# First stage: the transposes of the probabilities ahead of the projection of the values

## What is computed

```python
h = _layernorm(x) * (1 + ca) + sa          # per batch element
# attention: 16 heads of 64, window of 32 keys back
xn = rms_norm(h); q, k, v = split(xn @ w_qkv.T)
q, k = apply_rope(q), apply_rope(k)
attn = softmax(where(0 <= q_pos - k_pos <= 32, q.k / 8, NEG))
x = x + ga * ((attn @ v) @ w_out.T)
```

## Time and profile before

| | |
|---|---|
| median of 3 runs | 1226.2 us (1223.17 to 1226.77) |
| profiled execution, span | 1223.0 us (no other time is given for it) |
| TensorE busy | 1102.8 us, 90% |
| VectorE busy | 971.2 us, 79% |
| ScalarE busy | 921.4 us, 75% |
| GpSimd busy | 854.5 us, 70% |
| mean granted TensorE clock | 0.942 |

### The profile page before, as it was taken

How to read it: one execution, slowest core, us unless ns; L and a number is a source line. 1 busy time by engine, 2 the same in 40 slices (tenths; PEclk the granted TensorE clock), 3 DMA queues, 4 the chain that set the end, 5 groups by cost and what they waited for, 6 DMA issues and landing times. The chain is left out here.

```text
span 1223.0 us, 49591 instructions
## 1 busy us (share of the span) xinstructions
PE 1102.8 (90%) x17489; PEld 902.1 (74%) x17489; DVE 971.2 (79%) x4190; ACT 921.4 (75%) x3404; POOL 854.5 (70%) x685
## 2 busy tenths in 40 slices
PE   4899999999999999999999999947999984599992
PEld 2688888888888888888888887725787773488882
DVE  6898998898898898988989987546788764188884
ACT  2689989989889899899899898836776752366661
POOL 2777877877877878777878776554576677067775
PEclk9899999999999999999999999969988885699996
DMA  6766666766666666667667667352243123676110
GB/s 197 208 166 167 177 169 164 182 166 168 175 167 170 177 167 170 176 156 183 166 170 175 163 156 188 96 184 80 62 137 103 55 81 135 172 196 178 58 37 22
DMA packets 111026, 180.88 MB, mean 148 GB/s; under 512 B 19726, under 2 KB 64177, under 8 KB 110656
## 3 DMA queue, kind: packets, MB, share of 16 engines
q1 hardware_dynamic: 102944, 158.53, 50.3%
q0 software_dynamic: 6400, 16.82, 3.8%
q10 hardware_dynamic: 1440, 2.36, 0.8%
HBM read 35.20 MB, written 24.73 MB: 49 GB/s over the span
## 5 line engine op out<-in xcount | busy, mean ns | idle before, releaser
L612 POOL TENSOR_TENSOR qk<-mm,sw 128x1024 f32<-128x1024 f32 x128 | 305.0, 2383 | 96.2 <-DMA sw<-mm 96.1
L685 ACT ACTIVATE pr<-sm,mn 128x96 f32<-128x96 f32 x1024 | 368.6, 371 | 0.0
L618 POOL TENSOR_TENSOR pr<-pr,ri 128x768 f32<-128x768 f32 x128 | 189.1, 1478 | 73.0 <-DVE ri L540 72.9
L501 DVE TENSOR_TENSOR mm<-bank,cos 128x512 f32<-128x512 f32 x256 | 175.3, 685 | 69.9 <-PE bank L324 58.8
L685 ACT ACTIVATION_READ_ACCUMULATOR pr<-sm,mn 128x1 f32 x1024 | 202.2, 197 | 0.0
L513 DVE CUSTOM_DVE_ANT_0 sm<-bank,msk 128x96 f32<-128x96 f32 x1024 | 190.9, 252 | 3.4 <-PE bank L350 3.4
L502 DVE TENSOR_TENSOR mm<-bank,sin 128x512 f32<-128x512 f32 x256 | 174.0, 680 | 0.0
L377 PE MATMUL bank<-pT,vw 96*64 96x64 f32 x4096 | 147.5, 225 | 0.0
L377 PEld LDWEIGHTS bank<-pT,vw 96*64 96x64 f32 x4096 | 129.8, 138 | 17.1 <-issue 5.8
L676 ACT ACTIVATE pT<-bank 96x512 f32<-96x512 f32 x256 | 137.4, 588 | 0.5 <-PE bank L392 0.5
L392 PE MATMUL bank<-ident,pr 128*96 128x128 f32 x1024 | 133.6, 274 | 0.0
(11 more groups left out here) (206 smaller groups left out, 2492.8 us busy)
## 6 DMA issues: line engine op xcount, KB each, us to landing
sw<-mm SPq DMA_DIRECT2D x512, 128.0 KB, 2.4
vw<-vn SPq DMA_DIRECT2D x128, 192.0 KB, 2.6
vw<-vn SPq DMA_DIRECT2D x128, 128.0 KB, 2.3
rr<-sorted_scratch SPq DMA_DIRECT2D x72, 192.5 KB, 2.8
vw<-vn SPq DMA_DIRECT2D x96, 64.0 KB, 2.2
xt<-in_x SPq DMA_DIRECT2D x16, 256.0 KB, 3.9
x_scratch<-x SPq DMA_DIRECT2D x16, 256.0 KB, 2.5
rr<-x_scratch SPq DMA_DIRECT2D x16, 256.0 KB, 3.1
```

Of the source, the lines that this page charges most:

```text
L501: dve.tensor_tensor(mm[s % 2][:, 0, j, :], PJ[u % 2][:, :], cos[:, :], ALU.mult)
L612: pool.tensor_tensor(qk[i % 2][:, :, 32:], mm[i % 2][:, 0, :, :], sw[i % 2][:, :, :], ALU.add)\
L618: pool.tensor_tensor(t, t, ri[i % 2][:, :].unsqueeze(2).to_broadcast([P, 8, WK]), ALU.mult)\
L685: ins = act.activation(pr[i % 2][:, h, p, :], ms_[i % 2][:, h, p, :], ACT.Exp, scale=-1.0, bias=mn[i % 2][:, h, p:p + 1], accum_out=sums[i ...
```

## The change

In TensorE's loop steps 6 and 7 of the slot change places: the transposes of unit s-4 come directly behind the value products of unit s-5, and `values(s)` comes last. The waits stay with their steps, and the other engines' lists are as before.

```diff
                         ins.then_inc(s_pv, 1)
-                    if s < NI:
-                        values(s)
                     i = s - LT
                     if 0 <= i < NI:
                         pe.wait_ge(s_nm, i + 1)
...
                             for p in range(4):
                                 ins = pe.transpose(TR[h][0:WK, p * P:(p + 1) * P], pr[i % 2][:, h, p, :], ident[:, :])
                             ins.then_inc(s_tr, 1)
+                    if s < NI:
+                        values(s)
```

## The result

The changed kernel takes 1259.4 us (median of 4 runs, 1256.2 to 1262.6) against 1225.3 us (4 runs): 1.028 times the time of before, 95% interval 1.0255 to 1.0306. It is 34 us slower; 43 were forecast. (The forecast started from 1226.2 us, the median of three runs of the kernel before; a fourth brings it to 1225.3.)

What follows compares the result with a forecast made beforehand. TensorE's stream was taken to bound the first stage; 112 x 0.26, 15 x 0.57 and 15 x 0.38 us gave 43.4 us, on the 1226.2 us median: 1269 us. Range of 8 in 10: 1242 to 1284 us.

Steps and rivals of the forecast that it cites:

- Waits of the moved transposes: Transposes on TensorE, going 0.7 us earlier, still find their inputs from GpSimd and ScalarE ready: 0 us.
- Hand-overs on TensorE: Switches between kinds of matmul: each before has its like after, taken as 0; bounds +0.11 and -0.19 us per unit.
- The copy of the values: Second rope projection waits for ScalarE's copy to free its bank: 1.18 us needed, 0.92 available, 0.26 us stall per unit.
- the third rival: No change: ScalarE's copy stays hidden behind rope 0's three streams, by bank rotation; 1226 us, chance 0.04.
- ScalarE between two copies: Unit with the squares: ScalarE needs 6.40 us against 6.02, so 0.38 us more in 15 units; 0 in other units.
- the fifth rival: Loss spreads: late ScalarE may stop TensorE at a second place, value products waiting for pT; 1283 us and above, chance 0.09.
- The unit with x_high: Slot s % 8 = 6: rope 0 waits 0.57 us for VectorE's xl, replacing the 0.26 at rope 1; 15 units.
- What else moves: vw transfers issue some 0.9 us later, but they and GpSimd's sw transfers have enough slack: 0 us.
- The sum: Whole kernel: 29.1, 8.6 and 5.7 us together 43.4 us, giving 1269 us, 3.5% slower; second stage untouched.
- The second rival: Cheaper hand-overs on TensorE, -0.19 us in 128 units, pay for part of the stall: 1245 us, chance 0.12.
- the fourth rival: Faster, by a cheaper hand-over directly behind the value products, needing 0.37 us in 128 units: 1222 us or less, chance 0.05.
- The signs: Expected in the changed profile: L322 waiting for vn over 100 times, L377 wait staying, 6.02 us between value products.

Runs made afterwards that it cites:

- run 1: Changed kernel with the output projection moved between the two rope projections of the next unit: 1246.1 us against 1223.8 for the kernel before, ratio 1.0177.
- run 2: Kernel before, transposes still last, with the output projection moved between the two rope projections: 1224.4 us against 1223.8 for the kernel before, ratio 1.0006.
- run 3: Changed kernel with only the first head's four transposes ahead of the projection of the values: 1231.7 us against 1223.8 for the kernel before, ratio 1.0067.
- run 8: Kernel before with four of eight transposes ahead of the values' projection, only in slots s % 8 of 0, 1, 2, 6, 7: 1220.2 us, ratio 0.9968.
- run 5: Changed kernel with ScalarE's copy of the values cut from 512 to 256 columns: 1237.5 us against 1223.2 for the kernel before, ratio 1.0106.
- run 6: Kernel before with ScalarE's copy of the values cut to 256 columns: 1226.6 us against 1223.2 for the kernel before, ratio 1.001.
- run 4: Changed kernel with the output projection between the two rope projections and xh made between the two heads' exponentials: 1232.5 us, ratio 1.0075 to the kernel before.
- Run 7: Changed kernel with only xh made earlier, between the two heads' exponentials on ScalarE: 1254.2 us against 1223.2 for the kernel before, ratio 1.0252.

## Why the prediction was right

It was right in direction, mechanism and range; its size was 9 us too large, 5 of them by one term, the hand-overs.

*Waits of the moved transposes: 0.* Right. They follow the value products in 1.08 us, as the projection did in 1.09 (424.09 to 425.17; 429.13 to 430.22).

*Hand-overs on TensorE: taken as 0.* This is the term that was mis-sized. From the value products to the stream of rope 0 it took 431.89 - 429.13 = 2.76 us before (431.81 and 0.08 of slow start) and takes 426.78 - 424.09 = 2.69 to 2.70 now. The loads show where. First the kernel before, the two loads behind the value products' (whose own row is in the earlier trace rows):

```profile
407.19 0.19 PEld L298 LDWEIGHTS bank<-wh,xh 128*128 128x128 f32 x1
407.30 0.19 PEld L299 LDWEIGHTS bank<-wl,xh 128*128 128x128 f32 x1
```

then the changed kernel, the eight loads as one row, the first and the second of them alone, and the projection's:

```profile
425.17 0.83 PEld L390 LDWEIGHTS bank<-ident,pr 128*96 128x96 f32 x8
...
425.17 0.12 PEld L390 LDWEIGHTS bank<-ident,pr 128*96 128x96 f32 x1
...
425.21 0.13 PEld L390 LDWEIGHTS bank<-ident,pr 128*96 128x96 f32 x1
...
425.98 0.19 PEld L298 LDWEIGHTS bank<-wh,xh 128*128 128x128 f32 x1
426.09 0.19 PEld L299 LDWEIGHTS bank<-wl,xh 128*128 128x128 f32 x1
```

In both kernels the first load starts 0.07 us after the value products' last one ends. To the second load it is then 0.11 us before and 0.04 now, which is the whole difference. From the first transpose's load to the projection's stream it is 426.09 - 425.17 = 0.92 us, where I had reckoned 0.11 + 0.87 = 0.98. "Every hand-over before has its like after" was the step that failed: they have a like, not an equal.

The trace of before could have told. The nearest row that the prediction took was the yt transposes behind the scores, and it read there the 0.12 us ahead of the first load. But the value products' loads come as late behind the scores (411.04 + 0.70 = 411.74, next at 411.87), so that gap belongs to the scores. What belongs to the transposes is the distance to their second load, 0.06 us instead of 0.11:

```profile
411.04 0.70 PEld L350 LDWEIGHTS bank<-qk 64*64 64x64 f32 x32 [0.36 <-issue]
411.87 1.01 PEld L377 LDWEIGHTS bank<-pT,vw 96*64 96x64 f32 x32
...
399.76 0.14 PEld L360 LDWEIGHTS bank<-ident,yt 128*128 128x128 f32 x1
...
399.82 0.25 PEld L360 LDWEIGHTS bank<-ident,yt 128*128 128x128 f32 x2
```

Runs 1 and 2 show the 0.06 us without any stall, runs 3 and 8 some 0.04 to 0.05 of it. In the six intervals of a batch element that neither the squares nor xl set, 6.02 was forecast and 5.96 measured for a plain unit, so it makes 6 x 0.06 = 0.36, and that is about what is missing between the forecast's 2.77 us a batch element (7 x 0.26 + 0.57 + 0.38) and the measured 49.63 - 47.20 = 2.43. Over 15 batch elements: 5 us of the 9.

*The copy of the values: stall 0.26.* Right: 1.18 needed and 0.92 there by the forecast, 1.19 and 0.93 measured. Shown by taking the stall away with more cover (run 1), by shortening the copy (run 5), and by both edits doing nothing where the slack was (runs 2 and 6). The rotation of groups over different banks, which the Trainium skill asks for (Perfetto Trace Analysis, Matmuls), was in place with two banks before and after, and did not decide; start and release of the copy, 0.43 + 0.05 us on top of its 0.60, did. So the third rival fell.

*ScalarE between two copies: the squares unit at 6.40.* Right (6.40, then 5.96, which is a plain unit of this kernel). The second place of the fifth rival was there too, TensorE waiting for pT 12 times, 2.0 us in all, but it lies inside the unit that ScalarE sets, and cost nothing in the changed kernel. In runs 1 and 4, with the ordinary stall gone, the lateness behind the squares was not given back, and otl came up as a new wait; these two runs were 13 and 11 us slower than I expected.

*The unit with x_high: 0.57 at rope 0.* Right: 5-6 and 6-7 together take 12.86; before they took 12.09, and with the ordinary stall and the 0.57 that makes 12.09 + 0.26 + 0.57 = 12.92. The loads of that unit:

```profile
407.50 0.19 PEld L300 LDWEIGHTS bank<-wh,xl 128*128 128x128 f32 x1
408.48 0.19 PEld L322 LDWEIGHTS bank<-xh,wh 128*128 128x128 f32 x1 [0.79 <-DVE xl L426]
```

The load comes 0.98 us after that of L300, where 0.23 is plain, and its stream 0.11 after it, where 0.23 is plain: (0.98 + 0.11) - (0.23 + 0.23) = 0.63 us of stall at rope 0, where 0.57 was forecast. Run 7 took the wait away.

*What else moves: 0.* Right in the steady part: GpSimd waits 54.2 us for sw between 100 and 700 us, 59.6 before. Near the end it isn't: from the copy of unit 123 to the next it takes 10.31 us, 7.92 before. There the transfers for the second stage are in SP's queue. GpSimd and TensorE wait as follows in the changed kernel, 780 to 800 us:

```profile
POOL qk L612 <- DMA sw<-mm: 12.8, 4, 5.4
...
PE bank L350 <- POOL qk L612: 2.8, 1, 2.8
```

and in the kernel before, 745 to 762 us:

```profile
POOL qk L612 <- DMA sw<-mm: 9.2, 3, 5.0
...
PE bank L350 <- POOL qk L612: 2.1, 1, 2.1
```

Why these 2.4 us are more was not tried, and they can't be put down to the change: in run 2, whose total is unchanged, this interval is 11.45, and in runs 5 and 7, which have all eight transposes ahead, it is 8.17 and 8.40.

*The sum.* At the last copy the loss is 814.5 - 775.4 = 39.1 us, forecast 43.4. From there to the end of the span it is 445.0 us, 447.6 before. Among the kernels here, which all share the second stage, this stretch lies between 442.6 and 448.1, so these 2.6 us ask for no cause in the change. Together 36.5 us of span and 34 of the medians. From the forecast's 43.4 to the 34.1 measured it is thus 5 us less for the hand-overs, 2.4 more at unit 123, 2.6 less behind the last copy, and 2.4 less because the medians lie closer than the two profiled spans; some 1.6 are not placed. Only the first of these is a term of the forecast.

The second rival (cheaper hand-overs pay for part) was true in kind and a third of its size, 0.06 for 0.19. The saving sits at the place that the fourth rival named, directly behind the value products, and not between the two groups of wide matmuls. As a gain in all the fourth fell: it needed 0.37 a unit by its own count, and still 43.4 / 128 = 0.34 by the forecast's sum.

*The signs.* L322 waits for vn in 107 places of the whole trace (over 100 were named), 0.42 us each in a plain unit, and a plain unit takes 5.96 and not 6.02. One sign was wrong: ScalarE's wait for the value products (L377) was to stay, and it shrank. Between 100 and 700 us, before and then changed:

```profile
ACT oth L696 <- PE bank L377: 34.5, 64, 1.0
...
ACT oth L696 <- PE bank L377: 7.5, 24, 0.4
```

The prediction's own working had it right, with the idle time of a unit "all ahead of the copy now".

## What to carry to other kernels

When a group's bank is wanted again soon, count from its last matmul: start of the copy, its length, the release and an uncovered load, and compare with the matmuls that lie between. What lies behind the group and ahead of the bank's next user is cover. Here eight transposes were worth 0.26 us a unit more there than in front of the group. That the engine which sets the pace is full and shows no waits says nothing of how much slack its partners have; here the same reorder that lost 2.8% gained 0.3% once half of it was made, in only those units where the copy's engine had slack.

## What was not expected of the hardware

- Behind 32 small matmuls in quarters of the array the second weight load of the next group starts 0.04 us after the first where they load for transposes of 128 x 96, 0.06 us for transposes of 128 x 128 (yt, behind the scores), and 0.11 us for the wide matmuls' 128 x 128. So the size alone doesn't make it; why transposes get away with less is not shown. Later ones of the eight or four transposes come at 0.11 us each either way.
- A stall of 0.26 us in each unit leaves TensorE's busy share at 611.7 of 620 us, since the records' modelled ends cover it; the number of matmuls in the stretch fell by 4.8%.
